# Two graph layers with the same four sheets, a larger ring of gathered tiles and one landing count per four tiles

## The chip, the cores and the metric

The kernel runs on one core of one Trainium2 chip. The metric is the device time of one execution in microseconds (us). The kernel before takes 5256.29 us, the median of three runs (5254.63 to 5257.71).

## What is computed

A graph of 12500 nodes with 256 features each and 200000 edges goes through two graph layers, then the nodes go through a mixture of eight experts. The edges come sorted by destination, and a destination's number of edges falls with its number (`dst` is drawn as 12500 · u²), so that the first nodes have many edges and the last few. Cut to what matters:

```python
def _hconv(x, src, dst, ew, w1, b1, w2, b2, g, b):
    h = relu(x @ w1 + b1)
    agg = segment_sum(ew[:, None] * h[src], dst, num_segments=12500)
    return relu(_bn(agg @ w2 + b2, g, b))

h = _hconv(layernorm(x), ...c1...); h = relu(_bn(h, ...bn1...))
h = _hconv(h, ...c2...);            x = x + relu(_bn(h, ...bn2...) + layernorm(x))
# experts: for each of 8, W1, bn, relu, W2, bn, relu, Wo, weighted by a gate
x = x + _ffn(layernorm(x))
```

## The kernel before

**Stages.** `first_layer` (the norm, x @ w1, the preparation of the edge lists), `aggregate(0)` (the segment sum of layer 1 and the product with w2), `second_layer` (norm and the next x @ w1), `aggregate(1)`, then the experts. All is written out by hand, engine by engine: each engine has its own list of instructions in program order, and the lists meet only at semaphores. The change is in the two `aggregate` stages, of which the second is told here.

**Groups and tiles.** The edges are cut into 391 groups of 512, each of GT = 4 tiles of 128. A *gathered* group goes as follows. POOL fetches the 128 source rows of each tile with one indirect DMA of 128 KB (`gather`, L1054) into a slot of a ring of R = 16 tiles (`wst`, `f_xr`, `f_u`, four groups). DVE builds for each tile a weighted one-hot matrix (`onehots`, L1306) in a ring of RO = 12 tiles (three groups), two groups ahead. PE multiplies the rows by the one-hots (L1138, per group 8 products, 16 MATMUL records in the trace) into a bank (`ps` or `px`) and counts `g_mm`. DVE adds the bank to `agg` (L1420). POOL waits before each group's first gather until `g_mm` says that the group four back is multiplied (L1053); DVE waits before the one-hots of a group until the group three back is. PE waits for the one-hots, for the bank and, tile by tile, for the gathers: each ring slot has its own semaphore `ga`.

**Sheets.** The first groups, 124 in layer 1 and 140 in layer 2, are not gathered. Their edges stand as columns of dense matrices ("sheets", `front`) which PE multiplies with all of `h` in *units*: one unit is one of 98 blocks of 128 nodes, two products (L1106, four MATMUL records), into `pf`. SP loads the blocks of `h` (L1027) and of the sheet (L1029) for four blocks at a time, 25 times for each sheet, into two buffers in turn. The sheets are made in the first place they can be: four in layer 1, and the fifth (16 groups, 64 "hot" tiles) in layer 2. Making takes per tile four PE products (L1092), two DVE instructions (L1317, L1339), ACT instructions (L1203 to L1216) and stores.

**The planner.** `place(level)` says behind which gathered group q a unit stands on PE. It gives each group a room of `level` less `other[q]` (the group's own products, the hot tiles, 560 for the chunks once past `ZERO_Q`), and puts units, `cost` each, while room is left. `level` starts at 4000 and rises by 20 until the last unit stands ahead of `UNITS_END`. The first sheet's `cost` is 4 · (3 + 330 // 6 · 5) = 1112, and a group's own products are 16 · 111 = 1776.

**Chunks.** When nodes are complete, chunks of 512 of them are multiplied by w2 (L1115), with work on ACT and DVE (L1365, L1373), behind the groups.

Of the kernel before, what the change touches and what calls it, by code (L numbers as in the profile page):

```python
def build(nc, a, out):
# [8 lines left out]
    P = 128  # L10
# [85 lines left out]
    def sem(name):  # L96
        return top.enter_context(nc.semaphore(name))
# [38 lines left out]
    W_LAST = [SHEET[made[-1]][1] for made in MADE]  # L136
    CLEARS = 4
    A_W = [NHG * HG * max(SHEET[i][1] for i in made) for made in MADE]
    UPPER = [AW - x for x in A_W]

# [14 lines left out]
    with top:  # L155
# [600 lines left out]

        def gathered_value(layer, t):

            return 16 * (layer * len(range(t % R, NTL[0], R)) + t // R + 1)

# [157 lines left out]
        def aggregate(layer):  # L918
# [3 lines left out]
            with ExitStack() as s:  # L922
                G = ([w[:, k, :] for w in wst for k in range(KC)] + [xr[:, j, :] for j in range(TPC)]
                     + [u[:, k, i * C:(i + 1) * C] for k in range(KC) for i in range(CH // C)])
                assert len(G) == R
                OH_all = sb(s, f"oh{layer}", [P, RO, P])
# [11 lines left out]
                steps = sb(s, f"steps{layer}", [P, WIN_W])[:, :]  # L938

                made_g = range(HOT_G[layer][0], FGL[layer]) if layer else range(FGL[0])  # L940
                ew_parts = sb(s, f"ew_parts{layer}", [P, 2 * GT * len(made_g)])[:, :].rearrange("p (h j f) -> p h j f", h=2, j=GT)
                AH = [sb(s, f"ah{layer}_{i}", [P, KC, CH], f32r) for i in range(2)]
# [4 lines left out]
                HW = [AH[0][:, :, :].rearrange("p k n -> p (k n)")[:, 0:WIN_W]] + [  # L947
                    sb(s, f"hw{layer}_{i}", [P, WIN_W], f32r)[:, :] for i in range(2)]
                RH = len(HW)
# [54 lines left out]
                with nc.Block() as block:  # L1004
                    @block.sync
                    def _(g):
                        if layer == 0:
                            g.wait_ge(window_st, 16 * FB)
                        lo = HOT_G[layer][0] if layer else 0
                        n = GT * (FGL[layer] - lo)  # L1010
                        g.dma_start(window_row[:, 0:n], window_dram[lo:FGL[layer], :].rearrange("(o f) j -> o (f j)", o=1)).then_inc(
                            window_in, 16)

# [33 lines left out]
                    @block.gpsimd  # L1047
                    def _(g):
                        def gather(t):
                            e = F0[layer] + t  # L1050
                            col = e % GT * TW + e // GT
                            if t % GT == 0 and t >= R:
                                g.wait_ge(g_mm, E0 + t // GT - RG + 1)  # L1053
                            g.indirect_dma_start(G[t % R], None, h_dram[layer], bass.IndirectOffsetOnAxis(  # L1054
                                ap=src_col[:, col:col + 1], axis=0)).then_inc(ga[t % R], 16)

                        g.iota(steps, pattern=[[1, WIN_W]], base=0, channel_multiplier=0,
                               allow_small_or_imprecise_dtypes=True).then_inc(steps_set, 1)
                        for t in range(NT_):
                            gather(t)  # L1060
                        g.wait_ge(g_mm, E0 + NQ)

                        def tile(q, j):
                            g.tensor_copy(far_idx[:, :], src_col[:, bass.ds(q + j * TW, 1)]).then_inc(far_sem["idx"], 1)
                            take(g, "idx")
                            gathered = far_sem["gathered"]
                            g.indirect_dma_start(G[0], None, h_dram[layer], bass.IndirectOffsetOnAxis(
                                ap=far_idx[:, :], axis=0)).then_inc(gathered, 16)
                            g.wait_ge(gathered, 16)
                            g.dma_reset(range(gathered.num, gathered.num + 1))  # L1070
                            g.sem_clear(gathered)
                            g.sem_inc(far_sem["landed"], 1)
                            take(g, "added")

                        turns(g, tile=tile)
                        g.nop()

                    @block.tensor
                    def _(g):
# [48 lines left out]
                        for q in range(NQ):  # L1128
                            g.wait_ge(g_oh, E0 + q + 1)
                            if bank_of[q] in bank_of[0:q]:  # L1130
                                g.wait_ge(g_add, E0 + max(x for x in range(q) if bank_of[x] == bank_of[q]) + 1)
                            elif q >= 2:
                                g.wait_ge(hot_a, H0 + NHOT[layer])
                            for k in range(KC):
                                for t in tiles_of[q]:
                                    if k == 0:
                                        g.wait_ge(ga[t % R], gathered_value(layer, t))
                                    ins = g.matmul(pS[bank_of[q]][:, k, :], G[t % R][:, k * P:(k + 1) * P], OH[t % RO],  # L1138
                                                   start=t == tiles_of[q][0], stop=t == tiles_of[q][-1])
# [37 lines left out]
                    def _(g):  # L1177
# [41 lines left out]

                        clear(0)  # L1220
                        g.wait_ge(ew_set, 2 * layer + 2)
                        lows(0)
# [3 lines left out]
                        clear(1)  # L1226
                        ends = [seg_end(layer, m) for m in range(len(made))]
# [26 lines left out]

                        for m in (len(made) - 2, len(made) - 1):
                            g.wait_ge(hot_f[m % 2], hot_f_value(layer, m))
                        g.wait_ge(hot_p, H0 + NHOT[layer])
                        for k in range(KC):
                            g.activation(upper[k][:, free_w:], zero_col[:, :].broadcast_to([P, A_W[layer] - free_w]),
                                         ACT.Copy).then_inc(agg_set, 1)  # L1260

# [36 lines left out]
                    def _(g):  # L1298
# [88 lines left out]
                        ew_made = ew_col[:, :].rearrange("p (j g) -> p j g", g=TW)[:, :, made_g[0]:made_g[-1] + 1]  # L1387
                        g.tensor_copy(ew_parts[:, 0, :, :].bitcast(f32r), ew_made).then_inc(ew_set, 1)
                        g.wait_ge(ew_set, 2 * layer + 1)
                        g.tensor_tensor(ew_parts[:, 1, :, :], ew_made, ew_parts[:, 0, :, :], ALU.subtract).then_inc(ew_set, 1)  # L1390
                        g.wait_ge(steps_set, layer + 1)
                        g.memset(OH_all[:, :, :], 0.0).then_inc(oh_set, 1)
                        for t in range(RH - 1):
                            hot_rows(t)
                        g.wait_ge(oh_set, layer + 1)
                        for q in range(AG):
                            onehots(q)
                        for q in range(NQ):
# [13 lines left out]
                            if free_w and q == FREE_Q[layer]:  # L1412
                                g.wait_ge(agg_set, FREE_SET)
                            if q == ZERO_Q[layer]:
                                g.wait_ge(agg_set, UPPER_SET[layer])
                            if q == 0:
                                g.wait_ge(window_in, 16 * (layer + 1))
                                if layer == 0:
                                    g.wait_ge(agg_set, LOWER_SET)
                            g.tensor_tensor(win, win, pS[bank_of[q]][:, :, 0:wide], ALU.add).then_inc(g_add, 1)  # L1420
# [872 lines left out]
```

## Time and profile before

| | us |
|---|---|
| median of three runs | 5256.29 |
| the profiled execution's span | 5228.2 |
| outside the span (median less span) | 28.1 |
| first layer | 0 to 175 |
| gathers of layer 1, first to last start | 175.3 to 1779.0 |
| gathers of layer 2, first to last start | 1928.7 to 3397.0 |
| experts | about 3424 to 5228 |

The profiled execution has no total time of its own shown beside its span, so its time is taken as the span and what lies around it, 28.1 us. In the rows, PE is the matmul engine, PEld its weight loads, DVE the vector engine, ACT the scalar engine, POOL the engine that issues the gathers, SP the one that issues the loads. "Remote" as a releaser is a semaphore event that the trace doesn't tie to one instruction; "issue" is time in which the engine waited for nothing that the profile shows. A row by stretch gives the stretch, its length, busy us and number of records for PE, PEld, DVE, ACT and POOL, the granted clock of PE as a share of 2.4 GHz, the busy share of the DMA engines and GB/s. A row of a group of instructions gives count, busy us and mean ns of one, then the idle us just before them and what ended it; one of a line gives count, shortest, median and longest ns, and the first and the last start.

### The profile page before, as it was taken

To read this page: it belongs to the slowest core of one execution; us is meant where nothing else is said; L and a number is where in the kernel's file an instruction comes from. 1 tells how busy PE (TensorE), PEld (TensorE's weight loads), DVE (VectorE), ACT (ScalarE), POOL (GpSimd) and SP (SyncE) were. 2 spreads that over 40 slices of the span, in tenths; PEclk is the share of its full clock that TensorE was granted. 3 is DMA by queue.
4 is the path that set the end of the run, shared out by engine and by line. 5 is a ranking of instruction groups with operands and counts; after the bars stand their busy time and mean duration, and the time that the engine had idled before them with its cause. 6 is when DMAs were issued, how large, how long until landed. Compare 5 with 4: busy or idle time off the path is not lost. (4 is left out here: it accounts for less than half of the span.)

```text
span 5228.2 us, 71544 instructions
## 1 busy us (share of the span) xinstructions
PE 4623.3 (88%) x25508; PEld 3800.6 (73%) x25508; DVE 2688.7 (51%) x6606; ACT 2435.6 (47%) x4218; POOL 2110.6 (40%) x2284
## 2 busy tenths in 40 slices
PE   6778888888999579888988988649999999999999
PEld 5667777666677467776666666548888888888888
DVE  7666666566333464522222222366666666666665
ACT  4655556666211263300000000057777777777777
POOL 1466666566666456666666666630000000000000
PEclk9889999999999789999999999779999999999999
DMA  5467777566755247876666666431111111001110
GB/s 155 148 210 271 243 240 245 188 211 217 236 198 201 77 141 268 277 243 218 218 219 205 226 212 224 131 96 25 30 28 33 33 33 33 24 26 33 33 28 15
DMA packets 546618, 770.23 MB, mean 147 GB/s; under 512 B 149720, under 2 KB 441411, under 8 KB 546262
## 3 DMA queue, kind: packets, MB, share of 16 engines
q1 hardware_dynamic: 328176, 382.01, 21.7%
q0 software_dynamic: 100944, 273.96, 16.4%
q10 hardware_dynamic: 117142, 109.65, 6.5%
q8 instruction: 206, 3.38, 0.3%
q14 instruction: 150, 1.23, 0.1%
HBM read 605.58 MB, written 147.26 MB: 144 GB/s over the span
## 5 line engine op out<-in xcount | busy, mean ns | idle before, releaser
L1106 PE MATMUL pf<-work 128*128 128x330 f32 (+4 forms) x3528 | 1251.9, 491 | 63.3 <-DMA work<-front 31.3
L1054 POOL DMA_INDIRECT wst<-h,src_col x1040 | 1000.3, 962 | 541.9 <-issue 275.0
L1106 PEld LDWEIGHTS pf<-work 128*128 128x128 f32 x3528 | 661.0, 197 | 402.2 <-issue 220.1
L2096 DVE TENSOR_TENSOR f_hl<-f_hf,f_hh 128x1024 fp32r<-128x1024 f32 (+1 forms) x400 | 479.7, 1199 | 636.3 <-ACT f_hf L1959 636.0
L1952 ACT ACTIVATE f_hh<-f_p,f_sh,f_sc 128x512 fp32r<-128x512 f32 (+1 forms) x800 | 571.7, 768 | 395.9 <-PE f_p L2194 394.5
L1273 ACT ACTIVATE ah<-agg 128x1024 fp32r<-128x1024 f32 (+1 forms) x50 | 51.8, 1037 | 1464.2 <-DVE agg L1420 1086.6
L1138 PEld LDWEIGHTS ps<-oh,wst 128*128 128x128 f32 x4160 | 543.4, 203 | 144.5 <-issue 99.6
L1138 PE MATMUL ps<-oh,wst 128*128 128x128 f32 x4160 | 560.7, 288 | 88.6 <-issue 55.1
L1054 POOL DMA_INDIRECT f_xr<-h,src_col x518 | 497.7, 961 | 282.8 <-issue 134.0
L1054 POOL DMA_INDIRECT f_u<-h,src_col x512 | 491.1, 959 | 260.5 <-issue 136.7
L1959 ACT ACTIVATE f_hf<-f_p,f_sh,f_sc 128x512 f32<-128x512 f32 (+1 forms) x800 | 572.5, 775 | 0.0
L1420 DVE TENSOR_TENSOR agg<-agg,ps 128x68 f32 (+25 forms) x378 | 99.3, 263 | 918.7 <-remote 604.0
L1339 DVE TENSOR_TENSOR agg<-agg,px 128x686 f32 (+5 forms) x560 | 399.3, 713 | 259.4 <-remote 107.7
L1306 DVE TENSOR_SCALAR oh<-lane,rel_col,ew_col 128x36 f32<-128x36 f32 (+27 forms) x2070 | 510.6, 337 | 0.0
L1420 DVE TENSOR_TENSOR agg<-agg,px 128x140 f32 (+20 forms) x140 | 40.5, 289 | 561.5 <-remote 428.6
L2108 DVE SCALAR_TENSOR_TENSOR f_x<-f_p,f_gate,f_x 128x256 f32<-128x256 f32 x784 | 324.4, 476 | 2.4 <-PE f_p L2249 2.4
L2249 PE MATMUL f_p<-Wo_hi,f_hh 128*128 128x256 f32 (+1 forms) x1568 | 317.4, 284 | 2.4 <-DVE f_x L2108 2.4
L2249 PE MATMUL f_p<-Wo_lo,f_hh 128*128 128x256 f32 (+1 forms) x1568 | 314.4, 282 | 0.0
L2249 PE MATMUL f_p<-Wo_hi,f_hl 128*128 128x256 f32 (+1 forms) x1568 | 314.2, 282 | 0.0
L2249 PEld LDWEIGHTS f_p<-Wo_hi,f_hh 128*128 128x128 f32 (+1 forms) x1568 | 250.8, 189 | 25.9 <-issue 11.1
L2194 PE MATMUL f_p<-f_hh,W_hi 128*128 128x512 f32 (+1 forms) x800 | 252.9, 397 | 1.2 <-ACT f_hf L1959 1.2
L2194 PE MATMUL f_p<-f_yh,W_hi 128*128 128x512 f32 (+1 forms) x800 | 248.1, 391 | 4.4 <-DVE f_yl L2047 2.4
(285 smaller groups left out, 7648.0 us busy)
## 6 DMA issues: line engine op xcount, KB each, us to landing
work<-h SPq DMA_DIRECT2D x216, 512.0 KB
work<-front SPq DMA_DIRECT2D x50, 924.0 KB
front<-agg ACTq DMA_DIRECT2D x12, 3300.0 KB
work<-front SPq DMA_DIRECT2D x50, 756.0 KB
work<-front SPq DMA_DIRECT2D x50, 660.0 KB
work<-front SPq DMA_DIRECT2D x50, 580.0 KB
front<-agg ACTq DMA_DIRECT2D x8, 2600.0 KB
work<-front SPq DMA_DIRECT2D x25, 832.0 KB
```

What stands on the lines that cost most here:

```text
L1054: g.indirect_dma_start(G[t % R], None, h_dram[layer], bass.IndirectOffsetOnAxis(ap=src_col[:, col:col + 1], axis=0)).then_inc(ga[t % R], 16)
L1106: ins = g.matmul(pF[:, k, 0:count * w].rearrange("p (s c) -> p s c", c=w), HB[a % 2][0:r, n, k * P:(k + 1) * P], x, start=b == 0, stop=b = ...
L1138: ins = g.matmul(pS[bank_of[q]][:, k, :], G[t % R][:, k * P:(k + 1) * P], OH[t % RO], start=t == tiles_of[q][0], stop=t == tiles_of[q][-1])
L1306: ins = g.tensor_scalar(OH[t % RO][:, 0:wide], lane[:, 0:wide], rel_col[:, col:col + 1], ew_col[:, col:col + 1], ALU.is_equal, ALU.mult)
L1339: g.tensor_tensor(v, v, x, ALU.add).then_inc(hot_a, 1)
L1420: g.tensor_tensor(win, win, pS[bank_of[q]][:, :, 0:wide], ALU.add).then_inc(g_add, 1)
L1952: ins = g.activation(hhi[l][q % 2][:, m, 0:nn], p[:, m, 0:nn], ACT.Relu, bias=shift[l][:, col], scale=scale[l][:, col])
L1959: ins = g.activation(hf[l][:, m, 0:nn], p[:, m, 0:nn], ACT.Relu, bias=shift[l][:, col], scale=scale[l][:, col])
L2096: g.tensor_tensor(hlo[l][q % 2][:, :, 0:nn], hf[l][:, :, 0:nn], hhi[l][q % 2][:, :, 0:nn].bitcast(fp32), ALU.subtract).then_inc(f_lo[l], 1)
L2108: ins = g.scalar_tensor_tensor(X1[0:r, j, :], p3[0:r, j, :], gate[c % 2][0:r, j, e:e + 1], X1[0:r, j, :], ALU.mult, ALU.add)
L2194: ins = g.matmul(o[:, m, 0:nn], ww[:, k, m * P:(m + 1) * P], xx[:, k, 0:nn], start=i == 0 and k == 0, stop=i == 2 and k == KC - 1)
L2249: ins = g.matmul(p3[0:r, j, :], x[:, k, j * P:j * P + r], w[:, k, :], start=n == 0 and k == 0, stop=n == 2 and k == KC - 1)
```

## The change

There is no fifth sheet. Layer 2 gathers 267 groups (1067 tiles), as layer 1 does, where it gathered 251 (1003 tiles), and makes nothing: its iota, hot products, clears, window load and stores are gone, and with 98 blocks of the fifth sheet, 392 MATMUL records. Its ring of gathered tiles has 24 slots (a new buffer `ring` for 8 more), so that POOL waits for the group six back. It rotates four banks from its first group on. In both layers `ga` has one semaphore for four tiles, and PE waits once per group, for all four, ahead of its first product. The ring of one-hots stays at 12. The preparation of front groups in the first layer, which ran over two blocks of 128 groups (FG = 140, FB = 2), runs over one (FG = 124, FB = 1).

```diff
-              (66, [(5, 3, 7)]),
-              (52, [(2, 2, 7), (6, 2, 8)])]
-    MADE = [[3, 2, 1, 0], [4]]
-    USED = [[3, 2, 1, 0], [3, 2, 1, 0, 4]]
+              (66, [(5, 3, 7)]),
+              ]
+    MADE = [[3, 2, 1, 0], []]
+    USED = [[3, 2, 1, 0], [3, 2, 1, 0]]
...
-    HOT_Q = [188, 48]
+    HOT_Q = [188, 0]
...
-        R, RO = 16, 12
-        RG, ROG, AG = R // GT, RO // GT, 2
+        R, RO = [16, 24], 12
+        ROG, AG = RO // GT, 2
+        RG = [r // GT for r in R]
-        ga = [sem(f"g_ga{i}") for i in range(R)]
+        ga = [sem(f"g_ga{i}") for i in range(max(RG))]
...
-                bank_of = [q % 2 if q <= hot_q[layer][-1] else q % 4 for q in range(NQL[layer])]
+                bank_of = [q % 2 if made and q <= hot_q[layer][-1] else q % 4 for q in range(NQL[layer])]
...
-                            if t % GT == 0 and t >= R:
-                                g.wait_ge(g_mm, E0 + t // GT - RG + 1)
-                            g.indirect_dma_start(G[t % R], None, h_dram[layer], bass.IndirectOffsetOnAxis(
-                                ap=src_col[:, col:col + 1], axis=0)).then_inc(ga[t % R], 16)
-                        g.iota(steps, pattern=[[1, WIN_W]], base=0, channel_multiplier=0,
-                               allow_small_or_imprecise_dtypes=True).then_inc(steps_set, 1)
+                            if t % GT == 0 and t >= ring:
+                                g.wait_ge(g_mm, E0 + (t - ring) // GT + 1)
+                            g.indirect_dma_start(G[t % ring], None, h_dram[layer], bass.IndirectOffsetOnAxis(
+                                ap=src_col[:, col:col + 1], axis=0)).then_inc(ga[t // GT % RG[layer]], 16)
+                        if made:
+                            g.iota(steps, ...).then_inc(steps_set, 1)
...
+                            g.wait_ge(ga[q % RG[layer]], gathered_value(layer, q))
                             for k in range(KC):
                                 for t in tiles_of[q]:
-                                    if k == 0:
-                                        g.wait_ge(ga[t % R], gathered_value(layer, t))
```

Where the instructions stand. The planner's code is not touched, but its input is. First PE at the start of `aggregate(1)`, before (`ps`, `px`: banks of gathered groups and of hot products; `pf`: the units' bank; `work`: the loads' buffers; `ah`, `hw`: operands of the hot products; x8: eight products, a whole group):

```order
L1570 UNCONDITIONAL_BRANCH
L1078 UNCONDITIONAL_BRANCH
L1138 MATMUL ps1_0<-oh1,wst 128x128 x8
L1092 MATMUL px1_0<-ah1_0,ah1_1 128x344 x4
L1106 MATMUL pf1<-work1 128x330 x2
L1092 MATMUL px1_1<-hw1_0,ah1_1 128x344 x4
L1106 MATMUL pf1<-work1 128x330 x2
```

The same place in the changed kernel:

```order
L1586 UNCONDITIONAL_BRANCH
L1090 UNCONDITIONAL_BRANCH
L1149 MATMUL ps1_0<-oh1,wst 128x128 x8
L1118 MATMUL pf1<-work1 128x330 x196
L1149 MATMUL ps1_1<-oh1,wst 128x128 x8
L1149 MATMUL px1_1<-oh1,f_xr 128x128 x8
L1149 MATMUL px1_1<-oh1,f_u 128x128 x8
L1149 MATMUL ps1_0<-oh1,ring1 128x128 x8
L1118 MATMUL pf1<-work1 128x290 x6
L1149 MATMUL ps1_1<-oh1,ring1 128x128 x8
```

Before, the 98 units of the first sheet stood behind groups 0 to 42, one to three behind each. Now all 98 (196 products) stand behind group 0, ahead of group 1; groups 1, 2 and 3 have none. With a level of 4000 and no hot tiles the room of a group is 4000 - 1776 = 2224, exactly two units of 1112, and at a room of exactly zero `place` gives the first group its room anew (`if q == first and not room`). The other three sheets' 294 units stand behind groups 4 to 230.

POOL at the start of `aggregate(1)`, before:

```order
L1570 UNCONDITIONAL_BRANCH
L1047 UNCONDITIONAL_BRANCH
L1057 IOTA steps 128x784
L1054 DMA wst<-h,src_col 128x256 x8
L1054 DMA f_xr<-h,src_col 128x256 x4
L1054 DMA f_u<-h,src_col 128x256 x4
L1054 DMA wst<-h,src_col 128x256 x8
```

And in the changed kernel:

```order
L1586 UNCONDITIONAL_BRANCH
L1058 UNCONDITIONAL_BRANCH
L1065 DMA wst<-h,src_col 128x256 x8
L1065 DMA f_xr<-h,src_col 128x256 x4
L1065 DMA f_u<-h,src_col 128x256 x4
L1065 DMA ring<-h,src_col 128x256 x8
L1065 DMA wst<-h,src_col 128x256 x8
```

The iota is gone, and a turn of the ring is 24 gathers long, not 16.

## Rows read from the trace of the kernel before

**Rows 1.** The page: span, busy time and share of each engine.

```profile
span 5228.2 us, 71544 instructions
PE 4623.3 (88%) x25508; PEld 3800.6 (73%) x25508; DVE 2688.7 (51%) x6606; ACT 2435.6 (47%) x4218; POOL 2110.6 (40%) x2284
```

**Rows 2.** Gathers (L1054) from 2280 to 3400: starts, idle time before, releasers.

```profile
L1054 POOL DMA_INDIRECT wst<-h,src_col x384: 943/947/1441, 2290.1 to 3393.2; - x192
L1054 POOL DMA_INDIRECT f_xr<-h,src_col x194: 943/947/1341, 2279.7 to 3397.0; - x194
L1054 POOL DMA_INDIRECT f_u<-h,src_col x192: 944/948/1319, 2285.1 to 3381.0; - x192
...
  issue: 211.2, 692
  remote: 160.5, 71
```

**Rows 3.** Busy us and records of each engine in stretches of layer 2.

```profile
2280.00:2700.00 420.00, 380.31 (x1864) 277.08 (x1863) 100.86 (x392) 12.88 (x13) 273.56 (x289) 0.95 0.65 221
3269.00:3400.00 131.00, 85.11 (x446) 70.13 (x445) 42.50 (x133) 12.07 (x13) 85.80 (x90) 0.78 0.43 132
```

**Rows 4.** Timeline of layer 2, two gaps of POOL and the DVE adds beside them.

```profile
2637.56 1.95 PE L1138 MATMUL ps<-oh,wst 128*128 128x128 f32 x16
...
2645.18 0.27 PE L1138 MATMUL px<-oh,f_xr 128*128 128x128 f32 x1 [0.32 <-issue]
2646.08 0.27 DVE L1420 TENSOR_TENSOR agg<-agg,ps 128x112 f32 x1 [7.36 <-remote]
2646.21 0.95 POOL L1054 DMA_INDIRECT wst<-h,src_col  x1 [2.54 <-remote]
2647.47 0.95 POOL L1054 DMA_INDIRECT wst<-h,src_col  x1 [0.31 <-issue]
...
2663.59 0.94 POOL L1054 DMA_INDIRECT wst<-h,src_col  x1 [2.65 <-remote]
```

**Rows 5.** All gathers of layer 2 (L1054, 1925 to 3400).

```profile
L1054 POOL DMA_INDIRECT wst<-h,src_col x504: 943/947/1625, 1928.7 to 3393.2; - x168
```

**Rows 6.** Timeline of the start of layer 2: POOL, and PE's first group and units.

```profile
1927.80 0.79 POOL L1057 IOTA steps<- 128x784 f32 x1 [9.48 <-POOLq L1570]
1928.74 1.01 POOL L1054 DMA_INDIRECT wst<-h,src_col  x1 [0.16 <-issue]
...
1939.26 2.50 PE L1138 MATMUL ps<-oh,wst 128*128 128x128 f32 x10 [0.36 <-DMA wst<-h,src_col]
...
1942.34 1.27 PE L1106 MATMUL pf<-work 128*128 128x330 f32 x4
...
1945.19 1.95 PE L1138 MATMUL ps<-oh,wst 128*128 128x128 f32 x16
```

**Rows 7.** PE by form, whole span: units of the first and the fifth sheet.

```profile
L1106 PE MATMUL pf<-work 128*128 128x330 f32 x776 | 253.0, 455 | 25.2 <-issue 16.7 <-DMA work<-front 8.2
...
L1106 PE MATMUL pf<-work 128*128 128x416 f32 x388 | 148.9, 527 | 4.7 <-DMA work<-front 4.6
```

**Rows 8.** DMA traffic from 1957 to 2010, in 40 slices.

```profile
GB/s 12 97 410 415 318 155 105 99 99 0 88 385 420 340 173 99 111 99 192 311 201 345 396 424 405 379 373 364 363 363 398 390 205 105 99 141 313 435 310 108
```

**Rows 9.** DVE by line, 0 to 175: instructions as wide as the front's two blocks.

```profile
L528 DVE SCALAR_TENSOR_TENSOR agg<-agg 128x1024 f32<-128x1024 f32 x1 | 1.2, 1225 | 0.0
L572 DVE TENSOR_SCALAR agg<-agg,seg_c 128x512 f32<-128x512 f32 x2 | 0.9, 482 | 0.0
```

**Rows 10.** Gathers of layer 1 (L1054, 175 to 1780).

```profile
L1054 POOL DMA_INDIRECT wst<-h,src_col x536: 943/949/2639, 175.3 to 1775.1; - x179
L1054 POOL DMA_INDIRECT f_xr<-h,src_col x267: 943/948/1344, 186.7 to 1779.0; - x134
...
  PE ps L1138: 119.4, 70
```

More of the change, by code:

```diff
@@ L755, in build, with gathered_value, landed @@
         z_out = sem("z_out")
-        def gathered_value(layer, t):
-            return 16 * (layer * len(range(t % R, NTL[0], R)) + t // R + 1)
+        def gathered_value(layer, q):
+            def landed(n, x):
+                return 16 * min(GT, NTL[n] - x * GT)
+            slot = q % RG[layer]
+            before = sum(landed(0, x) for x in range(slot, NQL[0], RG[0])) if layer and slot < RG[0] else 0
+            return before + sum(landed(layer, x) for x in range(slot, q + 1, RG[layer]))
         NFL = [NHG * len(used) for used in USED]
@@ L924, in aggregate @@
                      + [u[:, k, i * C:(i + 1) * C] for k in range(KC) for i in range(CH // C)])
-                assert len(G) == R
+                if R[layer] > len(G):
+                    more = sb(s, f"ring{layer}", [P, R[layer] - len(G), C])
+                    G += [more[:, i, :] for i in range(R[layer] - len(G))]
+                ring = R[layer]
                 OH_all = sb(s, f"oh{layer}", [P, RO, P])
@@ L936, in seg_cells @@
                     return upper[m % 2][:, a_w - NHG * HG * SEGS[made[m]][1]:a_w]
-                steps = sb(s, f"steps{layer}", [P, WIN_W])[:, :]
-                made_g = range(HOT_G[layer][0], FGL[layer]) if layer else range(FGL[0])
-                ew_parts = sb(s, f"ew_parts{layer}", [P, 2 * GT * len(made_g)])[:, :].rearrange("p (h j f) -> p h j f", h=2, j=GT)
+                steps = sb(s, f"steps{layer}", [P, WIN_W])[:, :] if made else None
+                made_g = range(min(HOT_G[layer], default=0), FGL[layer] if made else 0)
+                ew_parts = (sb(s, f"ew_parts{layer}", [P, 2 * GT * len(made_g)])[:, :].rearrange("p (h j f) -> p h j f", h=2, j=GT)
+                            if made else None)
                 AH = [sb(s, f"ah{layer}_{i}", [P, KC, CH], f32r) for i in range(2)]
@@ L947, in aggregate @@
                 HW = [AH[0][:, :, :].rearrange("p k n -> p (k n)")[:, 0:WIN_W]] + [
-                    sb(s, f"hw{layer}_{i}", [P, WIN_W], f32r)[:, :] for i in range(2)]
+                    sb(s, f"hw{layer}_{i}", [P, WIN_W], f32r)[:, :] for i in range(2) if made]
                 RH = len(HW)
@@ L1218, in lows @@
                             ins.then_inc(hot_l, 1)
-                        clear(0)
-                        g.wait_ge(ew_set, 2 * layer + 2)
-                        lows(0)
+                        if made:
+                            clear(0)
+                            g.wait_ge(ew_set, 2 * layer + 2)
+                            lows(0)
                         if layer == 0:
@@ L1253, in _ @@
                                 store(m)
[L1255 to L1260, printed above, removed]
+                        if made:
+                            for m in (len(made) - 2, len(made) - 1):
+                                g.wait_ge(hot_f[m % 2], hot_f_value(layer, m))
+                            g.wait_ge(hot_p, H0 + NHOT[layer])
+                            for k in range(KC):
+                                g.activation(upper[k][:, free_w:], zero_col[:, :].broadcast_to([P, A_W[layer] - free_w]),
+                                             ACT.Copy).then_inc(agg_set, 1)
                         def split(n):
@@ L1386, in _ @@
                                 some += [g.alloc_register(f"{name}{i}") for i in range(BATCH)]
[L1387 to L1391, printed above, removed]
+                        if made:
+                            ew_made = ew_col[:, :].rearrange("p (j g) -> p j g", g=TW)[:, :, made_g[0]:made_g[-1] + 1]
+                            g.tensor_copy(ew_parts[:, 0, :, :].bitcast(f32r), ew_made).then_inc(ew_set, 1)
+                            g.wait_ge(ew_set, 2 * layer + 1)
+                            g.tensor_tensor(ew_parts[:, 1, :, :], ew_made, ew_parts[:, 0, :, :], ALU.subtract).then_inc(ew_set, 1)
+                            g.wait_ge(steps_set, layer + 1)
                         g.memset(OH_all[:, :, :], 0.0).then_inc(oh_set, 1)
-                        for t in range(RH - 1):
-                            hot_rows(t)
+                        if made:
+                            for t in range(RH - 1):
+                                hot_rows(t)
                         g.wait_ge(oh_set, layer + 1)
@@ L1413, in _ @@
                                 g.wait_ge(agg_set, FREE_SET)
-                            if q == ZERO_Q[layer]:
+                            if made and q == ZERO_Q[layer]:
                                 g.wait_ge(agg_set, UPPER_SET[layer])
-                            if q == 0:
+                            if made and q == 0:
                                 g.wait_ge(window_in, 16 * (layer + 1))
-                                if layer == 0:
-                                    g.wait_ge(agg_set, LOWER_SET)
+                            if q == 0 and layer == 0:
+                                g.wait_ge(agg_set, LOWER_SET)
                             g.tensor_tensor(win, win, pS[bank_of[q]][:, :, 0:wide], ALU.add).then_inc(g_add, 1)
```

20 lines of the change are left out of this document (12 added, 8 removed).

## Prediction

> **What bounds the kernel now.** I read the page's busy shares first [rows 1]: PE at 88% looks like the bound, but that is a mean over stages. The changed stage is layer 2's aggregation, and there the question is which engine's pace the stage keeps. The view of the gather's line answers it [rows 2]. From 2279.7 to 3397.0 us POOL starts 770 gathers, one per (3397.0 - 2279.7) / 769 = 1.453 us, so 5.81 us for a group of four. A gather takes 0.947 us busy and 0.30 "issue" ahead of the next [rows 2, 4], so 1.253 us, or 5.01 a group; the rest is the 160.5 us of "remote" waits, 71 of them, at the wait for the ring. The stretches show that this pace does not follow PE's load [rows 3]: from 2280 to 2700 PE is busy 91% and POOL issues 289 gathers in 420 us (1.453 each); from 3269 to 3400, where the units are over, PE is busy 65% and it issues 90 in 131 us (1.456). So the stage is paced by the gathers and their waits; PE's, DVE's and ACT's work lies beside them.
>
> The timeline shows what the waits are like [rows 4]. POOL runs twelve gathers without a gap and then stands for 2.54 us, again 17.38 us later for 2.65 us, while the ring is full. 17.38 us for three groups is 5.79 a group. Both times the wait ends together with a DVE add (2646.08), and the add had stood 7.36 us, though the sixteen records of its bank had started at 2637.56 and take 1.95; PE meanwhile goes on in single records with gaps of 0.32 between. So the news of a finished group comes late while gathers are in flight, and comes when they have landed. The run of twelve is three groups: the ring's four less the one in hand, but also the ring of one-hots, three groups. The trace can't tell which of the two sets it, and that is the first thing to decide.
>
> **The sum, part by part.** I follow POOL from its first gather in layer 2 to its last, since what stands behind (3397.0 on) is the same in both.
>
> (1) More gathers. 1067, not 1003. The first 28 of them (the ring's 24, and group 0's four slots again) find room; 28 · 1.253 = 35 us. The other 1039 go at the steady pace. Which pace? From below 1.253, if no wait is left; from above what layer 2 showed while it made the fifth sheet, (2279.7 - 1928.7) / 233 = 1.506 [rows 2, 5]. I take 1.453, the pace of the 770 gathers with no hot tiles beside them, since neither a lighter PE [rows 3] nor, as I read the runs of twelve, a longer ring moves it while the one-hots' ring stays at three groups.
>
> (2) The block of 98 units. The order of the change puts the whole first sheet behind group 0 on PE. PE works in order, so group 1 and all behind it stand until 98 · 4 = 392 records are through. Before, group 0 ended and the first unit began at 1942.3 [rows 6]. A unit's four records take 1.27 us with the last one's tail, so one per (1.27 - 0.455) / 3 = 0.27 us at best [rows 6, 7]: 392 of them 107 us. Over the whole span records of this form took 253.0 us busy and 25.2 us idle ahead of them for 776 [rows 7], 0.36 each: 141 us. I take the middle, 124 us: the best pace holds only when gathers are quiet, which they are after the first third. The loads don't set it: four blocks are 512 KB of h and 660 KB of the sheet, 1.2 MB, 3 us at the 400 GB/s that slices show [rows 8], against 4.4 to 5.7 us of PE for four units. So the block ends at about 1942 + 124 = 2066, and group 1, 1.95 us [rows 6], at 2068. POOL meanwhile has the ring full: it stands from 1928.7 + 35 = 1964 to 2068, about 104 us. Its next gather starts at 2068, the 29th; before, about the 93rd had started by then.
>
> Is the stand paid back? Only if something other than gathers paced the rest. PE has six landed groups and few units to do, so it catches up within a few groups; POOL then is the late one again, and its lost 104 us are lost. The last gather starts at 2068 + 1038 · 1.453 = 3576, against 3397.0: +179 us. Of this the 64 further gathers are 93 us and the block the rest.
>
> (3) What is taken away. The fifth sheet's 98 units and 64 hot tiles leave PE (392 records of L1106 and the products of L1092), DVE and ACT. All of it lay beside the gathers; I cost it at nothing, except that the hot stretch's slower pace (1.506 for 233 gathers, 12 us over 1.453) is already replaced in (1). If this cover were gone, that is, if PE paced the stage, the saving would be the fifth sheet's 149 us [rows 7] and more; what the stage then gains is bounded by the gathers' floor, which the rivals below reach. The iota, 0.79 us with its gap, is on the path: -0.9 us [rows 6].
>
> (4) The first layer. DVE prepares the front groups in instructions 1024 wide or twice 512 wide, from L528 (1.2) to L572 (0.9) and their like [rows 9]; there are ten such, of 0.7 to 1.4 us, 10.6 in all, and each halves: -5.3 us. Between nothing (if ACT or PE is late there) and that.
>
> (5) One wait per group. PE starts a group's products when the fourth tile has landed, not the first. Where PE is behind, this costs nothing. Where it waits for gathers, three tiles' first products (six records, 6 · 0.21 = 1.3 us) come after the last landing. On the path it stands at the end of each layer: 2 · 1.3 = +2.6 us. What is queued behind the wait on PE, units and chunks, has slack. Bound above by 15 us, should some groups hit it; below zero only if fewer waits let PE's news come earlier, a rival below.
>
> Sum: 179 - 0.9 - 5.3 + 2.6 = +175 us. From the profiled 5228.2 us to 5404 in the span, and with the same 28.1 us around it, 5432 us against the median of 5256.3.
>
> **A rule against this.** The row shows a gap that returns every 17.4 us [rows 4]. The Trainium skill, Perfetto Trace Analysis, Identifying Performance Opportunities, reads a gap that keeps repeating as possibly too few buffers in SBUF for the next tile. By that rule the ring is what is short, and 24 slots are the remedy; it is the second and third rival.
>
> **The rivals.** *The ring was the limit, partly.* If only the ring of gathers set the runs of twelve, a ring of six groups gives runs of twenty between gaps of the same size: 1.253 + (2.54 - 0.30) / 20 = 1.365 us a gather, 0.088 · 1038 = 91 us less than forecast, 5341 us. For it: the waits stand at the ring's full point. Against it: DVE's wait for the one-hots' ring, three groups, would stop PE at the same place.
>
> *The ring hides the waits whole (the other side).* If the news is late by a fixed time and not until all is quiet, two more groups of slack (10 us) cover gaps of 2.5 us and POOL runs at 1.253 to 1.30: 159 to 209 us less, 5223 to 5273 us. It decides from the point at which the news of group q is out before the gathers of q + 5 are. Half of this lies more than 0.2% (10.5 us, about what a measurement of this kernel can tell from no change) below 5256: faster, though the block is paid. For it: delays of 7 us against a slack of 20 us. Against it: the gaps end with the landings, and they are as large at 65% PE as at 91%.
>
> *PE's many waits were the cause.* If the wait for each tile is what holds PE's news, one wait per group frees both layers. Layer 1 issues 1067 gathers in 1779.0 - 175.3 us, 1.504 each, and part of its gaps are waits for PE's products in full (119.4 us at 70) [rows 10], so of 0.25 · 1066 = 267 us at most half to all comes back, on top of the last rival: 4960 to 5130 us. For it: PE's single steps while gathers fly. Against it: the same steps are there in units, which wait for no gather.
>
> *The block is not what I read,* because the loads or PE's clock make it longer or shorter: inside the range.
>
> **How the numbers follow.** Chances: forecast 0.65, with its own range 5410 to 5470 (the block 107 to 141 us, the pace up to 1.475 for the other 1038, first layer 0 to -5.3, waits up to +15); partly 0.12; whole 0.18, half of it below 5246 and a third within 0.2%; PE's waits 0.05. Faster by over 0.2%: 0.05 + 0.09 = 0.14. Within: 0.06. Slower: 0.80. The range of 8 in 10 leaves out the 0.05, the lower part of the whole rival and the forecast's far end: 5235 to 5465.
>
> **What would show it.** In the changed profile: 392 records of the 330-wide form without a gathered group between them, from about 1937 to 2060; POOL without a gather from about 1959 to 2063; after it 1039 gathers at 1.45 us with runs of twelve and gaps of 2.5. Layer 1 with first and last gather as far apart as before, 5 us earlier. Runs of twenty would show the partial rival, gaps gone the whole one; a layer 1 shorter by over 50 us the last. What would make the forecast wrong above all is a pace under 1.40 behind the block; wrong by less, a block off 124 us.

## The result, and the profile after

| | us |
|---|---|
| kernel before, median of four runs | 5255.46 (5250.58 to 5257.71) |
| changed kernel, median of four runs | 5432.39 (5426.76 to 5434.62) |
| ratio | 1.0335 (95% interval 1.0320 to 1.0349) |
| forecast | 5432 (5235 to 5465) |

Slower by 177 us, as forecast (175). Two warnings on the profiles first. The changed kernel's profiled execution has a span of 5432.8 us and took 5434.6, so only 1.8 us lie outside a span, not 28. And the kernel before is not equally fast on every chip: 5255.5 us (13 runs) on the one that ran the first four experiments, 5248.6, 5228.4 and 5223.4 on three others. The profile of before (span 5228.2) is like the last two; the medians above are like the first. So the two profiles differ by 205 us while the kernels, compared on one chip, differ by 177. Below, a stage is compared across chips only where nothing else is there, and each experiment's ratio is against runs of the kernel before on its own chip.

The page of the changed kernel, span and shares (for [rows 1]):

```profile
span 5432.8 us, 70221 instructions
PE 4635.9 (85%) x25101; PEld 3803.7 (70%) x25101; DVE 2606.6 (48%) x6539; ACT 2317.8 (43%) x3998; POOL 2168.2 (40%) x2343
```

The view of the gathers' line (L1065 now) in layer 2, for [rows 2, 5]: count, shortest, median and longest ns, first and last start, then POOL's idle time ahead of a gather by what ended it (us, times):

```profile
L1065 POOL DMA_INDIRECT wst<-h,src_col x360: 944/947/1427, 1933.4 to 3603.1; - x180
L1065 POOL DMA_INDIRECT f_xr<-h,src_col x179: 944/947/1327, 1943.5 to 3606.8; - x179
...
  issue: 300.5, 972
  remote: 213.0, 85
  PE ps L1149: 129.8, 3
```

From first to last gather are 3606.8 - 1933.4 = 1673 us. Of the 129.8 us in three waits on PE, 125.3 are the block; the kernel before has 28.2 us in 15 such waits. POOL's timeline at both ends of it and at the gaps behind it:

```profile
1967.28 0.95 POOL L1065 DMA_INDIRECT wst<-h,src_col  x1 [0.30 <-issue]
2093.48 0.95 POOL L1065 DMA_INDIRECT wst<-h,src_col  x1 [125.26 <-PE ps L1149]
...
2110.88 0.95 POOL L1065 DMA_INDIRECT ring<-h,src_col  x1 [2.68 <-remote]
...
2128.46 0.95 POOL L1065 DMA_INDIRECT wst<-h,src_col  x1 [2.86 <-remote]
```

POOL stands for 125.26 us, and then goes on just as before [rows 4]: twelve gathers, a gap of 2.7 to 2.9, 17.5 us from gap to gap. From 2093.5 to 3606.8 it starts 1038 gathers after the first, 1.458 us each. PE in the block, by form, from 1930 to 2100 (for [rows 7]):

```profile
L1118 PE MATMUL pf<-work 128*128 128x330 f32 x388 | 118.1, 463 | 25.7 <-DMA work<-front 25.7
```

388 records and four of the last, short block: 392 records, busy for 118.1 + 1.3 us, with 25.7 us idle ahead of them, all of it for the sheet's loads, in 14 waits. The timeline of PE and of SP shows the block's first part:

```profile
1943.04 3.75 PE L1149 MATMUL ps<-oh,wst 128*128 128x128 f32 x16 [15.35 <-DMA wst<-h,src_col]
1946.58 10.20 PE L1118 MATMUL pf<-work 128*128 128x330 f32 x32
1960.34 7.47 PE L1118 MATMUL pf<-work 128*128 128x330 f32 x16 [3.57 <-DMA work<-front]
1977.80 11.72 PE L1118 MATMUL pf<-work 128*128 128x330 f32 x32 [9.98 <-DMA work<-front]
```

```profile
1954.57 0.36 SPq L1038 DMA_DIRECT2D work<-h  x1
...
1972.19 0.36 SPq L1038 DMA_DIRECT2D work<-h  x1
...
1973.15 0.43 SPq L1038 DMA_DIRECT2D work<-h  x1
...
1985.11 0.36 SPq L1038 DMA_DIRECT2D work<-h  x1
...
1990.56 1.66 PE L1118 MATMUL pf<-work 128*128 128x330 f32 x5 [1.04 <-DMA work<-front]
```

A load issued at 1972.19 is multiplied from 1977.80, 5.6 us later; one issued at 1985.11 from 1990.56, 5.4 us later. And while gathers were in flight SP heard late that a buffer was free. Two buffers take turns, sixteen records each: the load of 1972.19 goes where the second sixteen records had read, and those ended at 1946.58 + 10.20 = 1956.8, so it was issued 15.4 us late; the load of 1973.15 waited for the sixteen that ended at 1967.8, 5.3 us late. The last gather had started at 1967.28, and the last packet of the gathers' queue ended at 1969.7. Later, with no gather in flight, the load of 1985.11 followed the end of its sixteen records at 1985.08 at once. So the 3.57 + 9.98 us of waits ahead of 1978 are mostly the late news, and the other twelve waits, 12.1 us, are the loads' own length against 4.4 to 4.7 us of products for four units. The block's end:

```profile
2088.94 2.49 PE L1118 MATMUL pf<-work 128*128 128x330 f32 x8 [0.80 <-DMA work<-front]
2091.26 1.95 PE L1149 MATMUL ps<-oh,wst 128*128 128x128 f32 x16
```

From 1946.6 to 2091.3 are 145 us.

### The profile page after: what moved, and what is told of

Same layout as the page of the kernel before. It is cut to its first block and busy times, and to the rows that moved or that the text cites. A ratio compares the mean times of both kernels' runs of the same rounds, so it can differ in the third digit from the quotient of the medians.

```text
span 5432.8 us, 70221 instructions
## 1 busy us (share of the span) xinstructions
PE 4635.9 (85%) x25101; PEld 3803.7 (70%) x25101; DVE 2606.6 (48%) x6539; ACT 2317.8 (43%) x3998; POOL 2168.2 (40%) x2343
## 5 line engine op out<-in xcount | busy, mean ns | idle before, releaser
L1118 PE MATMUL pf<-work 128*128 128x330 f32 (+4 forms) x3136 | 1168.7, 505 | 97.0 <-issue 61.5
L1065 POOL DMA_INDIRECT wst<-h,src_col x896 | 861.1, 961 | 602.0 <-issue 237.8
L1118 PEld LDWEIGHTS pf<-work 128*128 128x128 f32 (+1 forms) x3136 | 604.5, 204 | 401.6 <-issue 219.0
L1436 DVE TENSOR_TENSOR agg<-agg,ps 128x64 f32 (+27 forms) x362 | 95.5, 264 | 1059.7 <-remote 677.6
L1320 DVE TENSOR_SCALAR oh<-lane,rel_col,ew_col 128x34 f32<-128x34 f32 (+27 forms) x2134 | 528.7, 336 | 0.3
L1065 POOL DMA_INDIRECT f_xr<-h,src_col x446 | 427.6, 959 | 251.4 <-issue 116.0
L1065 POOL DMA_INDIRECT f_u<-h,src_col x440 | 423.4, 962 | 215.0 <-issue 122.0
L1149 PE MATMUL ps<-oh,wst 128*128 128x128 f32 x2880 | 406.0, 295 | 86.4 <-issue 50.3
L1149 PEld LDWEIGHTS ps<-oh,wst 128*128 128x128 f32 x2880 | 391.8, 210 | 122.7 <-issue 108.6
L1353 DVE TENSOR_TENSOR agg<-agg,px 128x686 f32 (+4 forms) x496 | 338.8, 683 | 222.0 <-remote 98.9
L1065 POOL DMA_INDIRECT ring<-h,src_col x352 | 335.6, 953 | 191.4 <-issue 98.7
```

Of the source, the lines that this page charges most:

```text
L1065: g.indirect_dma_start(G[t % ring], None, h_dram[layer], bass.IndirectOffsetOnAxis(ap=src_col[:, col:col + 1], axis=0)).then_inc(ga[t // G ...
L1118: ins = g.matmul(pF[:, k, 0:count * w].rearrange("p (s c) -> p s c", c=w), HB[a % 2][0:r, n, k * P:(k + 1) * P], x, start=b == 0, stop=b = ...
L1149: ins = g.matmul(pS[bank_of[q]][:, k, :], G[t % ring][:, k * P:(k + 1) * P], OH[t % RO], start=t == tiles_of[q][0], stop=t == tiles_of[q][-1])
L1320: ins = g.tensor_scalar(OH[t % RO][:, 0:wide], lane[:, 0:wide], rel_col[:, col:col + 1], ew_col[:, col:col + 1], ALU.is_equal, ALU.mult)
L1353: g.tensor_tensor(v, v, x, ALU.add).then_inc(hot_a, 1)
```

## The experiments

All are built on the changed kernel without its block (`a_spread`), unless said otherwise. "Pace" is the time from first to last gather of layer 2, a group of four.

**Without the block.** The planner's level starts at 4020, so that a group's room is 2244 and never exactly zero.

```diff
-            level = 4000
+            level = 4020
```

> The changed kernel with the planner's level starting at 4020, so that no room is exactly zero and the first sheet's 98 units stand two or three behind each group, not all behind group 0. Theory (the block holds POOL once, and nothing pays that back): POOL's stand of 125 us in layer 2 goes, 28 gathers at 1.253 and 1039 at 1.458 us make 1550 us from first to last gather in place of 1673, so 5309 us, 5300 to 5320. Rival (the stand was in part paid back, because six groups in hand let the rest run faster): the pace of the rest rises above 1.47 and the time stays above 5340 us.

Measured: 5323.6 us (5320.2 to 5331.9), ratio 1.0124 (1.0107 to 1.0141) against 5255.5, 4 us above the range expected and well below the rival's 5340. The block costs 109 us of the medians; forecast was 123 here, 104 in the prediction. In its profile:

```profile
L1065 POOL DMA_INDIRECT wst<-h,src_col x360: 942/946/1402, 1937.8 to 3489.1; - x180
L1065 POOL DMA_INDIRECT f_xr<-h,src_col x179: 944/946/1345, 1947.8 to 3492.8; - x179
...
  remote: 196.9, 73
```

1555 us from first to last gather, 118 less than with the block, and the pace, 5.84 us, is the one of the changed kernel behind the block (5.83). Nothing of the stand had been paid back within layer 2. What is left, 68 us over the kernel before, fits the 64 further gathers less the small gains (the prediction's sum without the block makes 72), but no run undoes them alone.

**Ring of 16 in layer 2**, the ring undone alone:

```diff
-        R, RO = [16, 24], 12
+        R, RO = [16, 16], 12
```

> a_spread with the ring of gathered tiles in layer 2 back at 16. Theory (DVE makes one-hots two groups ahead, so PE can be at most three groups past the last one it has reported, and POOL's runs are twelve gathers whatever the ring): within 10 us of a_spread, runs of 12 or 8. Rival (the ring of gathers sets the runs): slower by 40 us or more, with shorter runs.

Measured: 5312.3 us (5309.8 to 5326.3), ratio 1.0111 (1.0091 to 1.0131); pace 5.84, 70 runs of twelve in it where a_spread has 71. The larger ring does nothing: layer 2 takes 1556 us from first to last gather, against 1555. The difference of 11 us between the medians lies where both are the same code: of 19 us between the two spans 12 are in layer 1 (1613 us from first to last gather, against 1625) and 7 behind layer 2.

**One-hots three groups ahead**, with a ring of 16 of them in layer 2:

```diff
-        R, RO = [16, 24], 12
-        ROG, AG = RO // GT, 2
+        R, RO = [16, 24], [12, 16]
+        ROG, AG = [r // GT for r in RO], [2, 3]
...
```

> a_spread with the one-hots of layer 2 made three groups ahead, in a ring of 16 tiles, not two ahead in 12; four banks, so four groups can stand unreported. Theory (the one-hots' lead sets the length of a run between two quiet moments): runs of 16 and the same gap of 2.8 us, 1.253 + 2.5 / 16 = 1.41 us a gather in place of 1.458, 51 us less than a_spread, 5258 us. Rival (the ring, the gathers or DVE set it): no change, within 10 us of a_spread.

Measured: 5323.5 us (5318.0 to 5328.7), ratio 1.0128 (1.0111 to 1.0144), pace 5.83, 68 runs of twelve. My theory falls: the one-hots' lead doesn't set the runs either.

**Ring of 12 in layer 2**, three groups, the least that the one-hots' ring matches:

```diff
-        R, RO = [16, 24], 12
+        R, RO = [16, 12], 12
```

> a_spread with the ring of gathered tiles in layer 2 at 12, three groups. Theory (a run is three groups because PE reports three at each quiet moment; a ring of four groups is the least that lets POOL use them): POOL can be only three groups past the reported one, so runs of 8 with the same gap, 1.253 + 2.5 / 8 = 1.57 us a gather, 110 us more than a_spread, and landing times of tiles come on the path too. Rival (POOL's runs have nothing to do with the ring): as a_spread.

Measured: 5315.5 us, ratio 1.0123 (1.0094 to 1.0152), pace 5.83, 68 runs of twelve. Not 110 us more, but nothing. Between 12 and 24 slots the ring has no part in the pace, though PE now waits for gathers: in the view of who waited for them

```profile
  PE ps L1149: 108.1, 40
  PE px L1149: 77.2, 42
```

185 us in 82 waits, against one of 16.0 us in a_spread. They cost nothing.

**A quarter of the units' products in layer 2** (three quarters of that layer's sheet products left out; loads and all else stay), alone and with the one-hots three groups ahead:

```diff
+                            last = b == min((hg + 1) * HG, NB) - 1
+                            if layer and not last:
+                                return
...
```

> a_spread with only the last of each four units of layer 2 multiplied (98 of 392 units; the loads and all else stay; three quarters of layer 2's sheet products are left out of the result). In the cycles of a_spread PE is either busy or stepping through single records all the time, so its load may be what keeps a run at three groups. Theory A (PE's load sets the runs): runs of 16 and more, under 1.40 us a gather, at least 60 us less than a_spread. Theory B (whatever stops PE while gathers fly sets them): runs of 12 stay, within 15 us of a_spread.

> h_quarter_units with the one-hots of layer 2 made three groups ahead in a ring of 16. If PE's load and the one-hots' lead each hold runs at three groups, neither alone showed it, and the two together give runs of 16 and about 1.41 us a gather, 50 us less than h_quarter_units. If neither does, no change within 15 us.

Measured: 5306.5 and 5307.6 us, ratios 1.0106 (1.0077 to 1.0135) and 1.0108 (1.0079 to 1.0137): the longer lead adds nothing here either. The first against a_spread, from 2280 to 2700 (columns as in [rows 3]); a_spread:

```profile
2280.00:2700.00 420.00, 339.01 (x1698) 267.91 (x1698) 95.15 (x385) 8.93 (x9) 271.71 (x287) 0.88 0.56 184
```

and with a quarter of the units:

```profile
2280.00:2700.00 420.00, 264.90 (x1333) 216.75 (x1331) 92.14 (x376) 9.85 (x10) 276.01 (x291) 0.74 0.57 187
```

PE's busy share falls from 81% to 63%, and POOL issues 291 gathers in place of 287: pace over the layer 5.79 against 5.84, and 5.83 in m_ring12, which ran on the same chip as this one. But the runs did change: 33 of sixteen, 31 of twelve. Longer runs, the same pace: so the gaps are not what makes the pace. That is neither of the two theories, and I formed a third from it (C below): something behind the gathers takes 1.45 us for each, and the gaps are where POOL's faster issue is paid back.

**POOL made slower.** If C holds, work on POOL up to that rate costs nothing. A memset ahead of each group's gathers in layer 2, into a buffer that nobody reads (n_paced, 128x512; in o_paced_each ahead of every gather, 128x128; in q_paced_long ahead of each group, 128x1536):

```diff
+                            if layer and t % GT == 0:
+                                if t:
+                                    g.wait_ge(idled, t // GT)
+                                g.memset(idle[:, :], 0.0).then_inc(idled, 1)
                             gather(t)
...
```

> a_spread with a POOL memset of 128x512 ahead of each group's four gathers in layer 2, about 0.5 us busy, with its gap 0.5 to 0.8 us a group (133 to 214 us in all). Theory C (something behind the gathers drains at 1.45 us each, whatever POOL, the ring, the one-hots and PE do, and POOL's gaps are only where its faster issue is paid back): the gaps shrink by what the memsets take, the pace stays 5.83 us a group, within 15 us of a_spread. Theory D (each quiet moment costs 2.7 us for itself): the memsets come on top, 130 us or more over a_spread.

> a_spread with a POOL memset of 128x128 ahead of every gather in layer 2. Its length isn't known from a row; between 0.1 and 0.3 us with its gap gives gathers 1.35 to 1.55 us apart. Theory C: up to 1.45 apart the pace stays 5.83 a group with few gaps left, beyond it the pace is POOL's own with no gap. Theory D: the memsets' sum comes on top of a_spread whole, 107 to 320 us, and gaps of 2.7 us stay.

> n_paced with the memset ahead of each group 1536 wide, about 1.4 us busy, so that POOL's own sum is 5.0 + 1.3 = 6.3 us a group, above the 5.8 us at which layer 2 goes. Theory C (a pace of 1.45 us a gather set behind POOL): POOL is now the slowest, 6.3 us a group, (6.3 - 5.79) * 267 = 136 us more than n_paced and hardly a remote wait left. Theory D (quiet moments cost for themselves): more than 200 us over n_paced, with waits of the old size.

Measured, each ratio against runs of the kernel before on the same chip (5228.4 us beside the first two memsets, 5223.4 beside the third, 5255.5 beside a_spread):

| memset in layer 2 | POOL's own us a group | pace | runs' median | ratio to before |
|---|---|---|---|---|
| none (a_spread) | 5.01 | 5.84 | 5323.6 | 1.0124 (1.0107 to 1.0141) |
| 128x512 a group | 5.43 | 5.79 | 5291.8 | 1.0125 (1.0092 to 1.0157) |
| 128x128 a gather | 5.36 | 5.80 | 5291.5 | 1.0124 (1.0090 to 1.0157) |
| 128x1536 a group | 6.29 | 6.29 | 5413.2 | 1.0376 (1.0338 to 1.0414) |

The first two memsets cost nothing that can be seen: ratios within 0.0001 of a_spread's, with intervals of up to ±0.0034, about 18 us, where 267 times 0.42 us would be 112. The third costs 1676 - 1543 = 133 us between first and last gather against n_paced (on another chip), where 136 was expected; the ratios differ by 131 us. POOL's timeline with the memset a group, one full group:

```profile
2710.62 0.54 POOL L1077 MEMSET idle<- 128x512 f32 x1
2711.32 0.95 POOL L1067 DMA_INDIRECT wst<-h,src_col  x1 [0.17 <-issue]
2712.58 0.95 POOL L1067 DMA_INDIRECT wst<-h,src_col  x1 [0.30 <-issue]
2713.84 0.95 POOL L1067 DMA_INDIRECT wst<-h,src_col  x1 [0.30 <-issue]
2715.09 0.95 POOL L1067 DMA_INDIRECT wst<-h,src_col  x1 [0.31 <-issue]
2716.04 0.54 POOL L1077 MEMSET idle<- 128x512 f32 x1
2716.75 0.95 POOL L1067 DMA_INDIRECT wst<-h,src_col  x1 [0.17 <-issue]
```

5.43 us from group to group. The waits of the line that make up the rest, for n_paced and then for q_paced_long:

```profile
  remote: 82.3, 56
```

```profile
  issue: 288.1, 1061
  PE px L1155: 0.7, 4
  PE ps L1155: 0.3, 2
```

197 us of remote waits without a memset, 82 with the short one, none with the long. Theory D, a price for each quiet moment, would have put the memsets on top. It falls. C's rate stands in all three; where it is set the memsets don't tell (last section).

**PE's waits ahead of all products**, in the kernel before, both layers, nothing else:

```diff
+                            for t in tiles_of[q]:
+                                g.wait_ge(ga[t % R], gathered_value(layer, t))
                             for k in range(KC):
                                 for t in tiles_of[q]:
-                                    if k == 0:
-                                        g.wait_ge(ga[t % R], gathered_value(layer, t))
```

> The kernel before with PE's four waits for a group's tiles all ahead of its first product, in both layers; nothing else. Theory (the waits cost the first products of three tiles once a layer): 5255 + 3 us, within 5 us of the kernel before, and layer 1 from first to last gather 1604 us as before. Rival 1 (waits between products hold PE's news back): at least 50 us less. Rival 2 (the 18 us by which layer 1 was longer in the changed kernel's profile are the price of waiting for all four): 15 to 35 us more.

Measured: 5259.5 us, ten runs, against 5255.5, thirteen: ratio 1.0005 (0.9996 to 1.0015). Neither rival: the interval reaches from -2 to +8 us. Layer 1 took 1615 us from first to last gather; the other kernels took 1613 to 1625 on this chip, 1612 to 1620 on a second and 1593 to 1596 on two more. So the 18 us by which layer 1 is longer in the changed kernel's profile (1622) than in that of before (1604) are within what the chips and executions differ by, not a cost of the change.

**Hot tiles of layer 2 over 100 groups**, in the kernel before:

```diff
-    HOT_Q = [188, 48]
+    HOT_Q = [188, 100]
```

> The kernel before with the 64 hot tiles of layer 2 spread over its first 100 gathered groups, not 48. Theory (the gathers' 5.8 us a group is a floor, and only the dense hot stretch, 1.506 us a gather against 1.453, lies above it): spread out, the hot work fits under the floor, 5 to 12 us less than the kernel before. Rival (hot tiles cost the same wherever they stand): no change within 4 us.

Measured: 5225.8 us against 5223.4, ratio 1.0009 (0.9995 to 1.0022). No gain. Hot tiles slow the gathers wherever they stand, as the rival has it: layer 2's pace is 5.88 here, 5.86 in the profile of before. The slow stretch moved with them: before, the first 233 gathers go at 1.506 us and the next 187 at 1.459; here at 1.488 and 1.506; behind these both go at 1.451. That the price is the same for each tile isn't shown.

No kernel here beats the kernel before. Of those built on the changed kernel that compute the whole result, the nearest are those without its block (1.0111 to 1.0128), which still pay for 64 gathers more.

## Why the prediction was right, step by step

- **(1) 64 more gathers.** Right in size: 93 us forecast, and the kernel without the block is 68 us over before with all the small terms in it, where the sum makes 72. On one chip, layer 2 from first to last gather took 1484 us with five sheets (d_waits_first) and 1555 with four (a_spread), 71 more, where the sum makes 76. The steady pace was taken as 1.453 and measured 1.458. But the reason that I gave is wrong: I read the runs of twelve as set by the one-hots' ring, and ascribed the pace to run and gap. The runs are set by neither ring, and the pace is there without them. What did hold is the other half of the argument, that [rows 3] show one pace at two loads of PE.
- **(2) The block.** Right that it stands, that POOL stands with it, and that nothing pays it back. Mis-sized: 124 us forecast, 145 in the profile; POOL's stand 104 against 125. The failed step is "the loads don't set it": I took them by bandwidth, 3 us at 400 GB/s, where the timeline shows 5.4 to 5.6 us from issue to first product, and gave nothing for SP hearing late of a free buffer, up to 15.4 us, though I had read such lateness out of [rows 4]. 25.7 us of PE's time went there: 13.6 in two waits at the block's start, mostly the late news, and 12.1 in twelve later ones, the loads' length. PE's own work, 119.4 us, was inside the bounds. The upper bound, 141, was too low for this reason, by 4 us. Between medians the block's whole price is 109 us, while layer 2 alone shows 118 in the profiles. The profiles also differ behind layer 2: from the last gather to the end 1826 us in the changed kernel and 1837 in a_spread, where the code is the same and all the runs' profiles go from 1823 to 1841. Whether that is spread or a part given back isn't shown.
- **(3) What is taken away at no gain.** Right. Even with three quarters of the remaining units' products gone, the pace moves by little: 1543 us from first to last gather against 1553 in m_ring12 on the same chip.
- **(4) The first layer.** -5.3 forecast; the first gather of layer 1 stands at 167.3 where it was 175.3, and in the experiments at 165.7 to 168.0 with the change and 173.7 to 175.9 without: -8 us, -6 to -10 on one chip at a time. That the halved instructions are a part of it was not tested, and the rest wasn't traced.
- **(5) One wait per group.** +2.6 forecast, +4 measured with PE's four waits all ahead of the first product (d_waits_first), and not clear of nothing.
- **The sum.** 175 forecast, 177 between medians. That it is this near is luck: it came out nearer than its terms. Layer 2 is 205 us longer in the profiles where 179 was forecast, 21 of the difference in the block, and the forecast was made against a profile that is like those of faster chips than the one of the medians. The 28 us "outside the span" were not that, since a span and its time differ by 1.8 us; they were the chip. The range given for the forecast alone, 5410 to 5470, is also narrower than its terms: their ends added up make about 5412 to 5490.

The rivals: "the ring was the limit" and "the ring hides the waits whole" fall with the rings of 12, 16 and 24 at one pace, and with them, for this kernel, the rule that a gap that repeats may mean too few buffers (the Trainium skill, Perfetto Trace Analysis, Identifying Performance Opportunities): here the gaps repeat, 2.7 us in each 17.5, and twice the buffers change nothing. "PE's waits were the cause" falls with layer 1: with one wait for each group it takes 1613 to 1625 us on the chip on which it takes 1615 with four.

## What to carry to other kernels

A planner that fills rooms by subtraction is to be read for its edge cases each time its inputs change: two costs of 1112 fitted a room of 2224 exactly, and a test for "no room yet" took the zero for a fresh start, for 109 us. Before a ring is made longer, test whether the pace follows it at all: one run with a shorter ring, or with idle work on the issuing engine, tells whether its gaps are a cause or a symptom. And a load that stands alone ahead of its user is to be costed by its latency from the rows, not by its bytes, and by how late its issuer hears that the buffer is free.

## What the runs showed of the hardware that I had not expected

Gathers of 128 rows of 1 KB, issued by POOL at 1.253 us each, go at 1.447 to 1.460 us over the whole of layer 2, whatever the ring (12, 16, 24 tiles), the one-hots' lead (two or three groups), PE's load (63% or 81% busy) or up to 0.42 us of other work on POOL a group; with more work on POOL the rate is POOL's own. In the gaps POOL waits for a count from PE whose products had ended by the trace long before, and PE steps through single records, as in this stretch of the changed kernel from the first run behind the block:

```profile
2102.64 1.13 PE L1149 MATMUL ps<-oh,ring 128*128 128x128 f32 x7
2104.22 0.37 PE L1149 MATMUL ps<-oh,ring 128*128 128x128 f32 x1 [0.45 <-issue]
2105.63 0.27 PE L1149 MATMUL ps<-oh,ring 128*128 128x128 f32 x1 [1.04 <-issue]
2106.34 0.79 PE L1149 MATMUL ps<-oh,ring 128*128 128x128 f32 x2 [0.45 <-issue]
...
2110.75 3.11 PE L1118 MATMUL pf<-work 128*128 128x290 f32 x8
```

PE comes free at 2110.75, and POOL at 2110.88, together.

What it is that takes 1.45 us a gather stays open, but the traces narrow it. It is not POOL's issue. Nor is it the moving of the rows. In a_spread POOL starts twelve gathers from 2749.96 to 2763.72 and then stands until 2767.50. The row of the gathers' queue (packets, MB, share of the 16 engines) from 2751 to 2769, and from 2766 to 2769:

```profile
q0 software_dynamic: 576, 1.57, 27.6%
```

```profile
q0 software_dynamic: 8, 0.00, 0.1%
```

All twelve times 128 KB are moved by 2766.0, within 2.3 us of the start of the last gather. Over layer 2 of that trace, the last data packet of a gather ends 2.4 to 3.2 us after its start (medians by place in a run), and 2.4 us for the twelfth: nothing piles up along a run. The rows then lie waiting: PE starts a group's products 21.5 us (median) after its last gather's start with a ring of 24, and 5.1 us after with a ring of 12. What is late is the count: in a_spread POOL goes on 7.9 us (median) after the products of the group that it waits for had ended by the trace.

PE's idle time in layer 2 says the same. From 2280 to 3400, in a_spread, PE's largest:

```profile
PE px L1149 <- issue: 92.5, 124, 2.4
PE ps L1149 <- issue: 49.4, 73, 1.6
```

and in q_paced_long, where POOL's own 6.29 us a group set the pace, its largest and its largest of "issue":

```profile
PE px L1155 <- DMA wst<-h,src_col: 64.8, 23, 7.2
...
PE ps L1155 <- issue: 0.5, 2, 0.3
```

With the gathers at 1.45 us each PE steps through its records without waiting for any of them, 196 us of "issue" in all; at 1.57 us each the steps are gone, 0.8 us in all, and PE waits for gathers. PE has no landed groups in store then either, so that rate and store changed together. Whether the late counts cause the steps, or the steps the counts, or something behind both sets the 1.45 us, no run tells; gathers of fewer bytes or with fewer counts weren't tried.
